# A chunked delta-rule recurrence in a transformer kernel: the two batch rows half a chunk apart, the state kept in PSUM, preparation in smaller pieces, and opening state products at full array size

## Chip, cores and metric

The kernel runs on one core of a Trainium2 chip. The metric is the device time of one execution in microseconds (us), as the median of several runs; the profile is one further execution, taken by the hardware profiler. The engines are TensorE (PE, its weight loads PEld), VectorE (DVE), ScalarE (ACT), GpSimd (POOL) and SyncE (SP, which issues the DMAs).

## What is computed

A two-layer network in float32 over x of shape (2, 1024, 128). Its first part, which the change touches, is a gated delta-rule attention with 8 heads (keys of 64, values of 128). Its core is a scan over the 1024 steps:

```python
def step(S, ins):
    q_t, k_t, v_t, a_t, b_t = ins
    read = jnp.einsum('bhk,bhkv->bhv', k_t, S)
    err = read - v_t
    S = a_t[:, :, None, :] * S - b_t[:, :, None, None] * k_t[..., None] * err[:, :, None, :]
    o_t = jnp.einsum('bhk,bhkv->bhv', q_t, S)
    return (S, o_t)
```

q, k and v come from projections with a causal convolution of 4 taps and SiLU; a and b are sigmoids of projections; the output o is normalised per head, gated and projected. Mixture-of-experts layers, a softmax attention and layer norms follow, which the change leaves alone.

## The kernel before

**Stages.** An opening stage loads and prepares (0 to 71 us of the profile). The recurrence runs from 71 to 1304 us, a short closing stage to 1331 us, and the rest of the network to the end.

**Chunks and segments.** The 1024 steps are cut into 16 segments (f) of 64 steps, each of 4 chunks (c) of 16 steps, each of 4 blocks (i) of 4 steps. There are two batch rows (b = 0, 1); the 8 heads sit side by side in one tile. So there are 64 chunks of each row.

**One row's chunk.** `start` (L637, L644) puts the values and the products of keys and queries with the state into the PSUM bank z of the row. The state products use half of the columns of the array at a time: 8 matmuls with 64 columns of weights. Then come four block steps: `solve` on DVE multiplies z with the small inverse mt (L785) and sums it into w (L788); `turn` transposes w on PE (L653); `keep` on ACT copies 32 rows into wt (L746); `take_off` on PE (L662) takes the block's effect off the later blocks' z. After the fourth, `finish` makes the outputs (L669) and the keys-times-errors product (L677) in PSUM bank 4, one bank for both rows. `update` on DVE scales the outputs (L796), adds bank 4 to the state in SBUF (L799), and multiplies it by the decay (L803), which SP has loaded by DMA. The next chunk's `start` of that row waits for it.

**Products of the keys.** For each chunk and row, `pe_products` (L540, L542) makes the keys' products and their transpose in bank 5; DVE masks them into gq (L574, `dve_masks`) for `take_off` and the outputs, and ACT writes four scaled copies of the transpose into kfull (L552) for L677.

**The ring.** Between the steps of the recurrence the engines do the preparation of the next segment and the normalising, gating and projecting of the last one. The table BOTH has one slot for each of the 16 blocks of a segment, with two parts; a part names items, each one filling of a PSUM bank 6 or 7 by PE (`pe_item`) and its evacuation by ACT (`act_item`) or DVE. The fill of an item waits until the item two before it has been evacuated. a, b, k, q, v are projections (L333, L328), n products of neighbouring keys (L318), g, c, var, rs, wo, yt belong to the last segment.

**Queues.** Every engine works its instructions off in the order in which they are written. The order is written out by hand: for each chunk all four blocks of both rows alternate, with a ring part between them. DVE has its own share of the preparation in `prepare_slot` (L424 to L466), in whole-segment instructions of 256 to 1024 elements a partition; the inverse mt is its last part, ready (m_done) after the last chunk of the segment. POOL goes segment by segment: the scan of the decays (L501), near (L478), rstd, the copies of keys and queries into kq (L492), then the gate (L513, L516).

## Time and profile before

| | us |
|---|---|
| median of 3 runs | 2597.03 (2590.77 to 2597.59) |
| the profiled execution | 2591.12 |
| its span, first to last instruction | 2589.3 |
| the recurrence in it | 1232 (72 to 1304) |
| one segment of 4 chunks | 77 |

The profile shows each engine's busy time, the waits, and the instructions in order of time. PE's busy time counts a pipelined matmul's whole latency, so the distance from one start to the next is what a matmul costs its queue. Each float32 matmul is issued as two passes, a transpose as one; a count of 8 in a row of PE stands for 4 matmuls.

### The profile page before, as it was taken

To read this page: it belongs to the slowest core of one execution; us is meant where nothing else is said; L and a number is where in the kernel's file an instruction comes from. 1 tells how busy PE (TensorE), PEld (TensorE's weight loads), DVE (VectorE), ACT (ScalarE), POOL (GpSimd) and SP (SyncE) were. 2 spreads that over 40 slices of the span, in tenths; PEclk is the share of its full clock that TensorE was granted. 3 is DMA by queue.
4 is the path that set the end of the run, shared out by engine and by line. 5 is a ranking of instruction groups with operands and counts; after the bars stand their busy time and mean duration, and the time that the engine had idled before them with its cause. 6 is when DMAs were issued, how large, how long until landed. Compare 5 with 4: busy or idle time off the path is not lost. (4 is left out here: it accounts for less than half of the span.)

```text
span 2589.3 us, 44842 instructions
## 1 busy us (share of the span) xinstructions
PE 2260.6 (87%) x16524; PEld 1728.4 (67%) x16524; DVE 1531.3 (59%) x3305; ACT 1060.7 (41%) x2983; POOL 457.1 (18%) x868
## 2 busy tenths in 40 slices
PE   4888888888888888888849799999999999969997
PEld 3777777777777777777746556555556656666675
...
DMA packets 76174, 54.81 MB, mean 21 GB/s; under 512 B 6201, under 2 KB 72897, under 8 KB 74945
## 3 DMA queue, kind: packets, MB, share of 16 engines
...
q14 instruction: 73, 0.59, 0.1%
...
## 5 line engine op out<-in xcount | busy, mean ns | idle before, releaser
L1410 DVE TENSOR_REDUCE b_nmax<-ps 128x1 f32<-128x1024 f32 (+7 forms) x256 | 194.1, 758 | 325.0 <-PE ps L1310 324.2
L1306 PE MATMUL ps<-b_kT,b_qT 64*128 64x512 f32 (+3 forms) x768 | 327.8, 535 | 17.3 <-issue 15.4
L1377 ACT ACTIVATE b_prob<-ps,b_nmax 128x1024 f32<-128x1024 f32 (+7 forms) x256 | 189.7, 741 | 342.3 <-DVE b_nmax L1410 342.2
L785 DVE TENSOR_TENSOR prod<-ps,mt 128x128 f32<-128x128 f32 x512 | 148.4, 290 | 294.2 <-PE ps L662 242.7
L328 PE MATMUL ps<-xT,taps 128*128 128x128 f32 x2176 | 299.0, 280 | 0.6 <-ACT vd L379 0.6
L501 POOL TENSOR_TENSOR di<-di 128x128 f32<-128x128 f32 x240 | 130.4, 543 | 786.1 <-DVE di L430 768.5
L328 PEld LDWEIGHTS ps<-xT,taps 128*128 128x128 f32 x2176 | 265.1, 191 | 4.3 <-ACT vd L379 0.9
L653 PE MATMUL ps<-ident,w 128*128 128x128 f32 x512 | 159.7, 312 | 108.1 <-DVE w L788 106.6
L746 ACT COPY wt<-ps 32x128 f32<-32x128 f32 x512 | 129.3, 255 | 242.9 <-PE ps L653 235.4
L1306 PEld LDWEIGHTS ps<-b_kT,b_qT 64*128 64x128 f32 x768 | 127.2, 191 | 120.0 <-issue 103.2
L1039 PE MATMUL ps<-xTn,f_w 128*128 x352 | 167.4, 611 | 24.9 <-PEq L948 18.5
L1053 PEld LDWEIGHTS ps<-f_w,f_hT 128*128 128x128 f32 x1408 | 167.6, 193 | 31.6 <-issue 24.0
L1423 DVE COPY b_probT<-ps 128x512 f32<-128x512 f32 (+3 forms) x256 | 150.2, 587 | 62.0 <-PE ps L1332 60.8
L653 PEld LDWEIGHTS ps<-ident,w 128*128 128x128 f32 x512 | 75.4, 147 | 165.4 <-DVE w L788 161.9
L1332 PE MATMUL ps<-ident,b_prob 128*128 128x128 f32 x1152 | 175.3, 281 | 1.6 <-ACT b_prob L1377 0.9
L677 PE MATMUL ps<-wt,kfull 128*128 128x128 f32 x1024 | 147.7, 290 | 30.1 <-issue 30.1
L1053 PE MATMUL ps<-f_w,f_hT 128*128 128x128 f32 x1408 | 169.3, 277 | 0.8 <-DVE f_hT L1116 0.8
L552 ACT ACTIVATE kfull<-ps,pair_rows 128x128 f32<-128x128 f32 x520 | 162.9, 365 | 15.2 <-DVE gq L574 7.6
L1288 POOL COPY b_spread<-b_inv 128x128 f32<-128x128 f32 x128 | 38.0, 297 | 724.8 <-DVE b_inv L1430 724.8
L1349 PE MATMUL ps<-b_probT,b_v 128*64 128x128 f32 x2304 | 155.0, 279 | 4.5 <-DVE b_yT L1440 4.5
L677 PEld LDWEIGHTS ps<-wt,kfull 128*128 128x128 f32 x1024 | 132.1, 201 | 39.0 <-issue 38.7
L1332 PEld LDWEIGHTS ps<-ident,b_prob 128*128 128x128 f32 x1152 | 133.5, 144 | 35.8 <-issue 28.1
...
## 6 DMA issues: line engine op xcount, KB each, us to landing
decay<-ends_dram SPq DMA_DIRECT2D x256, 128.0 KB, 5.0
...
```

What stands on the lines that cost most here:

```text
L328: mm = pe.matmul(part, lhsT=taps[:, tap, t * P:(t + 1) * P], rhs=xT[:, :, columns(at_next) - LOOK + tap:columns(at_next) - LOOK + tap + TS ...
L552: nc.scalar.activation(kfull[:, B * (cc % 2) + b, g, :], ps[:, 5, KT_AT:KT_AT + P], ACT.Copy, scale=cst["pair_rows"][:, g:g + 1]).then_inc ...
L653: pe.transpose(ps[:, 2 + b, 0:P], w[:, b, :, :, :].rearrange("p i h s -> p (i h s)"), cst["ident"][:, :]).then_inc(wt_ready[b], 1)
L677: mm = pe.matmul(ps[:, 4, g * P:(g + 1) * P], lhsT=kfull[:, n % 4, g, :], rhs=wt[:, b, :], start=True, stop=True, skip_group_check=True)
L1039: pe.matmul(ps[:, m % 4, :], lhsT=w1[:, m * P:(m + 1) * P], rhs=xT[:, bass.ts(part(E // NE), 512)], start=True, stop=True).then_inc(sems[" ...
L1053: mm = pe.matmul(ps[:, 4 + e % 2, t * P:(t + 1) * P], lhsT=hT[:, e % 2, j, t * P:(t + 1) * P], rhs=w2[:, first[e] + j, :], start=(j == 0), ...
L1306: mm = pe.matmul(bank[:, 0:c1 - c0], lhsT=qT[rows, f, b * T + i * P:b * T + (i + 1) * P], rhs=kT[rows, f, b * T + c0:b * T + c1], start=Tr ...
L1332: mm = pe.transpose(ps[:, 4 + j // 4, (j % 4) * P:(j % 4 + 1) * P], prob[:, u % 2, j * P:(j + 1) * P], cst["ident"][:, :])
L1349: pe.matmul(ps[cols, 6, 0:P], lhsT=v[:, f, b * TT + j, cols], rhs=probT[:, (2 * w + h) % 4, j, :], start=(j == 0), stop=(j == i), skip_gro ...
L1377: nc.scalar.activation(prob[:, u % 2, 0:n], src, ACT.Exp, bias=nmax[:, u % 4:u % 4 + 1], accum_out=total[:, w % 4, h:h + 1]).then_inc(sems ...
L1410: nc.vector.tensor_reduce(nmax[:, u % 4:u % 4 + 1], src, axis=AX.X, op=ALU.max, negate=True).then_inc(sems["max_done"], 1)
L1423: nc.vector.tensor_copy(probT[:, u % 4, 0:k, :], ps[:, 4, 0:k * P].rearrange("p (j t) -> p j t", j=k)).then_inc(sems["pt_kept_v"], 1)
```

## The change

- The two rows are half a chunk apart. The loop runs over 128 half chunks, 8 to a segment (j = 0 to 7). In each, one row x makes its `start` and blocks 0 and 1, the other row y its blocks 2 and 3 and its `finish`.
- Each row has its own PSUM bank, 4 or 5, and the state stays in it: L677's products are added onto it (now L699), one DVE instruction multiplies bank by decay into SBUF (L827 takes the place of L799 and L803), and ACT copies the result back into the bank (`put_back`, L774, 128x512).
- The state products of `start` (now L668) are 4 matmuls with all 128 columns of weights instead of 8 with 64.
- The products of the keys are ring items p0 to p7, one to a half chunk. ACT copies their transpose once (kt), and POOL makes kfull from it in one 128x512 instruction with two inputs (L569).
- The ring has 32 parts, in another order. On DVE the preparation is cut in 22 pieces of half the size (`dve_piece`). The diagonal of mt goes from DVE (L438) to ACT, in two halves (L502), the scaling of the values from DVE (L461) to POOL (L510).
- POOL's work of a segment is spread over the halves: near in j = 1, the scan from j = 3, the gate in j = 5, the copies in j = 6, the values in j = 7, and a kfull ahead of each.

```diff
+        BOTH = [["k0.0"], ["k0.1"], ["k1.0"], ["k1.1", "p0"], ["a0"], ["c0"], ["a1"], ["c1", "p1"],
+                ["a2", "var.0"], ["var.1", "b0"], ["b1", "a3"], ["b2", "b3", "p2"], ["n0", "n1"], ["g0", "n2"], ["g1", "n3"],
+                ["p3"], ["rs0", "q0.0"], ["q0.1", "rs1"], ["q1.0"], ["q1.1", "p4"], ["v0.0"], ["v0.1"], ["v1.0"],
+                ["v1.1", "p5"], ["v2.0"], ["v2.1"], ["dt", "v3.0"], ["v3.1", "p6"], ["wo.0"], ["wo.1"], [], ["p7", "yt"]]
         POST = ("g0", "g1", "c0", "c1", "var", "rs0", "rs1", "wo", "yt")
+        PRODUCTS = tuple(f"p{j}" for j in range(2 * NC))
...
+            elif kind == "p":
+                cc, b = product_of(f, int(j))
+                if cc % NC == 0 and cc:
+                    pe.wait_ge(S["copied"], 16 * (cc // NC))
+                keys = kq[:, cc // NC % 2, b, cc % NC, :, :, :, :, :].rearrange("p q i g h s -> p (q i g h s)")
+                pe.matmul(out[:, 0:2 * P], lhsT=keys[:, 0:P], rhs=keys, start=True, stop=True, skip_group_check=True)
+                mm = pe.transpose(out[:, 2 * P:3 * P], keys[:, 0:P], cst["ident"][:, :])
...
+            elif kind == "p":
+                cc, b = product_of(f, int(j))
+                n = B * cc + b
+                act.wait_ge(S["g_kept"], n)
+                if n >= 3:
+                    act.wait_ge(S["k_kept"], n - 2)
+                last_one = nc.scalar.copy(kt[:, n % 2, :], out[:, 2 * P:3 * P])
...
+            if 8 <= q < 12 or 13 <= q < 16:
+                decays_piece(dve, ch, ring, f, nx, q - 8 if q < 12 else q - 13, 0 if q < 12 else 1)
+            if q in (12, 19):
+                rates_piece(dve, ch, ring, f, q // 19)
+            if 20 <= q < 25:
+                inverse_piece(dve, ch, ring, f, nx, q - 20, 0)
+            if 25 <= q < 30:
+                inverse_piece(dve, ch, ring, f, nx, q - 25, 1)
...
+            if step == 0:
+                wait_kept(dve, ring, f, "n3" if half else "n1")
+                dve.wait_ge(S["r_made"], 2 * f + half + 1)
                 ch.step(tt(NN[:, :, 0:3], NN[:, :, 0:3], R[:, :, 1:4], ALU.mult))
-            if slot == 12:
-                tt(NN[:, :, 3:5], NN[:, :, 3:5], R[:, :, 2:4], ALU.mult)
+                ch.step(tt(NN[:, :, 3:5], NN[:, :, 3:5], R[:, :, 2:4], ALU.mult))
+            if step == 1:
                 ch.step(tt(NN[:, :, 5:6], NN[:, :, 5:6], R[:, :, 3:4], ALU.mult))
-            if slot == 13:
-
-                nc.vector.scalar_tensor_tensor(out=M[:, :, 4:16:5], in0=NN[:, :, 0:3], scalar=-1.0, in1=R[:, :, 0:3],
-                                               op0=ALU.mult, op1=ALU.mult)
-
-                dve.wait_ge(S["copied"], 16 * (f + 1))
+                ch.step(stt(out=M[:, :, 4:16:5], in0=NN[:, :, 0:3], scalar=-1.0, in1=R[:, :, 0:3], op0=ALU.mult, op1=ALU.mult))
...
+        def act_diagonal(act, f, nx, half):
+
+            blocks = slice(half * HB * NBLK // 2, (half + 1) * HB * NBLK // 2)
+            act.wait_ge(S["r_made"], 2 * f + half + 1)
+            R = rr[:, :, :, :].rearrange("p h b (n i) -> p (h b n) i", i=BK)[:, blocks]
+            M = mt[:, nx, blocks, :, :].rearrange("p n i j -> p n (i j)")
+            nc.scalar.copy(M[:, :, 0:16:5], R).then_inc(S["diag_made"], 1)
+
+        def pool_values(pool, ring, f, nx):
+
+            wait_kept(pool, ring, f, "v3")
+            pool.wait_ge(S["d_done"], f + 1)
+            inv = di[:, 1, :, :]
+            vv = vd[:, nx, :, :, :].rearrange("p h b (c t) -> p (h b c) t", t=CH)
+            nc.gpsimd.tensor_tensor(vv[:, :, 1:CH], vv[:, :, 1:CH], inv[:, :, 0:CH - 1], ALU.mult).then_inc(S["prepared"], 1)
...
+        def pool_keys(pool, cc, b):
+            n = B * cc + b
+            if cc >= 2:
+                pool.wait_ge(p_ready[b], cc - 1)
+            nc.gpsimd.tensor_tensor(kfull[:, n % 4, :, :], kt[:, n % 2, :].unsqueeze(1).to_broadcast([P, G, P]),
+                                    cst["pair_rows"][:, :].unsqueeze(2).to_broadcast([P, G, P]), ALU.mult).then_inc(
+                S["k_kept"], 1)
...
-                        for half in halves_of_v:
-                            mm = pe.matmul(zo[half, :, g, :], lhsT=state[:, b, g, half],
-                                           rhs=kq[:, f % 2, b, c, :, :, g, :, :].rearrange("p q i h s -> p (q i) (h s)"),
-                                           start=False, stop=(g == G - 1), skip_group_check=True)
+                        mm = pe.matmul(zo[:, :, g, :], lhsT=state[:, b, g, :],
+                                       rhs=kq[:, f % 2, b, c, :, :, g, :, :].rearrange("p q i h s -> p (q i) (h s)"),
+                                       start=False, stop=(g == G - 1), skip_group_check=True)
...
+                    if n >= 1:
+                        pe.wait_ge(S["k_kept"], n)
                     if cc >= 1:
-                        pe.wait_ge(S["k_kept"], 4 * (nth(cc, b) + 1))
-                    for bb in range(B):
-                        if finished[bb]:
-                            pe.wait_ge(p_used[bb], finished[bb])
+                        pe.wait_ge(s_back[b], cc)
                     for g in range(G):
-                        mm = pe.matmul(ps[:, 4, g * P:(g + 1) * P], lhsT=kfull[:, n % 4, g, :], rhs=wt[:, b, :],
-                                       start=True, stop=True, skip_group_check=True)
+                        mm = pe.matmul(ps[:, 4 + b, g * P:(g + 1) * P], lhsT=kfull[:, n % 4, g, :], rhs=wt[:, b, :],
+                                       start=False, stop=True, skip_group_check=True)
                     mm.then_inc(p_ready[b], 1)
...
+                    y, cy = 1 - x, cc - 1 + x
+                    start(cc, x)
+                    if cy >= 0:
+                        turn(cy, y, 2)
+                    ring(0)
+                    if cy >= 0:
+                        take_off(cy, y, 2)
+                    turn(cc, x, 0)
+                    ring(1)
+                    take_off(cc, x, 0)
+                    if cy >= 0:
+                        turn(cy, y, 3)
+                    ring(2)
+                    turn(cc, x, 1)
+                    if cy >= 0:
+                        finish(cy, y)
+                    take_off(cc, x, 1)
+                    ring(3)
+                turn(last_chunk, 1, 2)
+                take_off(last_chunk, 1, 2)
+                turn(last_chunk, 1, 3)
+                finish(last_chunk, 1)
...
+                for cc, x, f, j in halves:
+                    nx = 1 - f % 2
+                    if j or f:
+                        of, oj = (f, j - 1) if j else (f - 1, 2 * NC - 1)
+                        wait_kept(pool, both, of, f"p{oj}")
+                        pool_keys(pool, *product_of(of, oj))
+                    if j == 1:
+                        pool_prepare(pool, both, f, nx, "near")
+                    if j == 3:
+                        pool_rstd(pool, ch, both, f)
+                        scan(ch, nc.gpsimd.tensor_tensor, f, nx)
+                    if j == 5:
+                        pool_gate(pool, ch, both, f)
+                    if j == 6:
+                        pool_prepare(pool, both, f, nx, 0)
+                        pool_prepare(pool, both, f, nx, 1)
+                    if j == 7:
+                        pool_values(pool, both, f, nx)
...
+                def put_back(cc, b):
+                    act.wait_ge(s_ready[b], cc + 1)
+                    nc.scalar.copy(ps[:, 4 + b, :].rearrange("p (g v) -> p g v", g=G), state[:, b, :, :]).then_inc(s_back[b], 1)
...
+                    y, cy = 1 - x, cc - 1 + x
+                    if cy >= 0:
+                        keep(cy, y, 2)
+                    ring(0)
+                    keep(cc, x, 0)
+                    if cc >= 1:
+                        put_back(cc - 1, x)
+                    ring(1)
+                    if j in (4, 6):
+                        act_diagonal(act, f, 1 - f % 2, j // 6)
+                    if cy >= 0:
+                        keep(cy, y, 3)
+                    ring(2)
+                    keep(cc, x, 1)
+                    ring(3)
...
+                def update(cc, b):
                     dve.wait_ge(p_ready[b], cc + 1)
-                    nc.vector.tensor_tensor(state[:, b, :, :], ps[:, 4, :].rearrange("p (g v) -> p g v", g=G),
-                                            state[:, b, :, :], ALU.add).then_inc(p_used[b], 1)
-                    dve.wait_ge(p_used[b], cc + 1)
                     dve.wait_ge(decay_in[b][cc % DS], 32 * (cc // DS + 1))
-                    nc.vector.tensor_tensor(state[:, b, :, :], state[:, b, :, :], decay[:, cc % DS, b, :, :],
-                                            ALU.mult).then_inc(s_ready[b], 1)
-
-                for cc, (f, c) in enumerate(chunks):
-                    def work(i):
-                        dve_slot(dve, ch, both, f, 1 - f % 2, NB * c + i, f - 1)
-
-                    solve(cc, 0, 0)
-                    solve(cc, 1, 0)
-                    work(0)
-                    solve(cc, 0, 1)
-                    dve_masks(dve, cc + 1, 0)
-                    solve(cc, 1, 1)
-                    work(1)
-                    solve(cc, 0, 2)
-                    solve(cc, 1, 2)
-                    work(2)
-                    solve(cc, 0, 3)
-                    dve_masks(dve, cc + 1, 1)
-                    solve(cc, 1, 3)
-                    prepare_slot(dve, ch, both, f, 1 - f % 2, NB * c + NB - 1)
-                    update(cc, 0)
-                    update(cc, 1)
-                    work(3)
-                    if c == NC - 1:
-                        prepare_slot(dve, ch, both, f, 1 - f % 2, 16)
+                    nc.vector.tensor_tensor(state[:, b, :, :], ps[:, 4 + b, :].rearrange("p (g v) -> p g v", g=G),
+                                            decay[:, cc % DS, b, :, :], ALU.mult).then_inc(s_ready[b], 1)
...
+                    y, cy = 1 - x, cc - 1 + x
+                    if cy >= 0:
+                        solve(cy, y, 2)
+                    solve(cc, x, 0)
+                    piece(0)
+                    if cy >= 0:
+                        solve(cy, y, 3)
+                    solve(cc, x, 1)
+                    piece(1)
+                    if cy >= 0:
+                        outputs(cy, y)
+                    piece(2)
+                    if cy >= 0:
+                        update(cy, y)
+                    dve.wait_ge(S["ring_done"], both.done(f, f"p{j}"))
+                    pc, pb = product_of(f, j)
+                    dve_masks(B * pc + pb, bank(both, f, f"p{j}"))
+                    piece(3)
```

**POOL, the recurrence, a segment in the middle.** Before, from the scan to the gate:

```order
L501 TENSOR_TENSOR di<-di 128x128 x15
L478 TENSOR_TENSOR near<-qk 128x128x3
L478 TENSOR_TENSOR near<-qk 128x128x2
L478 TENSOR_TENSOR near<-qk 128x128
L508 TENSOR_SCALAR rstd<-var 128x8
L509 TENSOR_TENSOR rstd<-rstd,minus_half 128x8
L492 COPY kq<-qk 64x8x4x4 x16
L513 TENSOR_SCALAR gate<-gate 128x1024
L516 TENSOR_TENSOR cs<-cs,gate 128x512 x2
```

The same engine now, from the scan (L544) to the values (L510); L535 are the copies, L556 and L559 the gate:

```order
L544 TENSOR_TENSOR di<-di 128x128 x15
L569 TENSOR_TENSOR kfull<-kt,pair_rows 128x512 x2
L556 TENSOR_SCALAR gate<-gate 128x1024
L559 TENSOR_TENSOR cs<-cs,gate 128x512 x2
L569 TENSOR_TENSOR kfull<-kt,pair_rows 128x512
L535 COPY kq<-qk 64x8x4x4 x16
L569 TENSOR_TENSOR kfull<-kt,pair_rows 128x512
L510 TENSOR_TENSOR vd<-vd,di 128x64x15
```

Eight kfull instructions and the values have come in, and the gate stands behind the scan and two of them.

**DVE, the end of a chunk in which part of the inverse is made.** Before:

```order
L788 TENSOR_REDUCE w<-prod 128x32
L438 COPY mt<-rr 128x256x4
L439 TENSOR_TENSOR gn<-gn,rr 128x256x3
L796 TENSOR_TENSOR vd<-ps,di 128x8x16
L799 TENSOR_TENSOR state<-ps,state 128x512
L803 TENSOR_TENSOR state<-state,decay 128x512
L796 TENSOR_TENSOR vd<-ps,di 128x8x16
L799 TENSOR_TENSOR state<-ps,state 128x512
L803 TENSOR_TENSOR state<-state,decay 128x512
```

Now, half chunk j = 5 of a segment, from its first piece of the inverse to the next half's first solve (L811, L814 are `solve`, L821 the outputs, L827 the update, L574 the masks):

```order
L477 TENSOR_TENSOR gn<-gn,rr 128x128x3
L478 TENSOR_TENSOR gn<-gn,rr 128x128x2
L811 TENSOR_TENSOR prod<-ps,mt 128x128
L814 TENSOR_REDUCE w<-prod 128x32
...
L483 TENSOR_TENSOR tmp<-gn,rr 128x128x2
L484 TENSOR_TENSOR tmp<-gn,mt 128x128x2
L827 TENSOR_TENSOR state<-ps,decay 128x512
L574 TENSOR_TENSOR gq<-ps,head_masks 128x256
L486 SCALAR_TENSOR_TENSOR mt<-tmp 128x128x2
L487 TENSOR_TENSOR tmp<-gn,rr 128x128
L811 TENSOR_TENSOR prod<-ps,mt 128x128
```

Each piece now stands between two solves, and one of them (L486, L487) between the masks and the half's first solve.

**PE, one row's start.** Before, two rows one behind the other; now one, followed by the other row's turn (L677 is now `turn`):

```order
L637 MATMUL ps<-vd,ident 128x128
L644 MATMUL ps<-kq,state 64x8x8 x8
```

```order
L662 MATMUL ps<-vd,ident 128x128
L668 MATMUL ps<-kq,state 128x8x8 x4
L677 MATMUL ps<-ident,w 128x128
```

The eight half-width products have become four of full width.

## Rows read from the trace of the kernel before

**Rows 1.** Windows: length; busy us of PE, PEld, DVE, ACT, POOL; clock, DMA share.
```profile
640.00:717.00 77.00, 66.94 (x563) 59.49 (x562) 53.66 (x120) 37.84 (x119) 22.19 (x38) 0.93 0.12 29
72.00:1304.00 1232.00, 1065.43 (x9055) 941.71 (x9054) 867.63 (x1936) 605.58 (x1904) 364.46 (x624) 0.95 0.13 29
```

**Rows 2.** Timeline of PE: runs of passes, each up to the next's start.
```profile
640.56 1.84 PE L286 MATMUL ps<-mean_col,gn 128*128 128x1 f32 x16
642.27 0.31 PE L653 MATMUL ps<-ident,w 128*128 128x128 f32 x1
...
647.63 0.69 PE L644 MATMUL ps<-kq,state 128*64 128x64 f32 x16
648.25 1.16 PE L328 MATMUL ps<-xT,taps 128*128 128x128 f32 x8
```

**Rows 3.** Waits in the recurrence: who waited for whom, us, times, longest.
```profile
DVE prod L785 <- PE ps L662: 242.7, 256, 2.5
DVE state L799 <- PE ps L677: 36.5, 80, 1.4
PE ps L653 <- DVE w L788: 106.6, 153, 2.1
```

**Rows 4.** Timeline, one block step: start, us, engine, line, instruction.
```profile
653.31 0.29 DVE L785 TENSOR_TENSOR prod<-ps,mt 128x128 f32<-128x128 f32 x1
653.64 0.29 DVE L788 TENSOR_REDUCE w<-prod 128x32 f32<-128x128 f32 x1
653.98 0.33 PE L653 MATMUL ps<-ident,w 128*128 128x128 f32 x1 [0.24 <-DVE w L788]
654.34 0.26 ACT L746 COPY wt<-ps 32x128 f32<-32x128 f32 x1 [0.28 <-PE ps L653]
656.09 0.31 PE L662 MATMUL ps<-gq,wt 128*128 128x32 f32 x2
656.43 0.29 DVE L785 TENSOR_TENSOR prod<-ps,mt 128x128 f32<-128x128 f32 x1 [0.79 <-PE ps L662]
```

**Rows 5.** Groups of the recurrence on DVE: count, busy us, mean ns, idle before.
```profile
L799 DVE TENSOR_TENSOR state<-ps,state 128x512 f32<-128x512 f32 x128 | 88.0, 688 | 36.5 <-PE ps L677 36.5
L574 DVE TENSOR_TENSOR gq<-ps,head_masks 128x256 f32<-128x256 f32 x128 | 54.1, 422 | 8.5 <-PE ps L542 7.9
L445 DVE SCALAR_TENSOR_TENSOR mt<-gn,rr 128x768 f32<-128x768 f32 x16 | 24.7, 1542 | 0.0
L441 DVE TENSOR_TENSOR gn<-gn,rr 128x512 f32<-128x512 f32 x16 | 14.0, 873 | 0.0
L442 DVE TENSOR_TENSOR gn<-gn,rr 128x256 f32<-128x256 f32 x16 | 10.1, 633 | 0.0
```

**Rows 6.** Timeline of DVE and POOL where both read SBUF.
```profile
53.34 1.00 DVE L439 TENSOR_TENSOR gn<-gn,rr 128x768 f32<-128x768 f32 x1
...
657.93 2.78 POOL L513 TENSOR_SCALAR gate<-gate 128x1024 f32<-128x1024 f32 x1 [1.72 <-DVE cs L403]
...
660.55 1.12 DVE L438 COPY mt<-rr 128x1024 f32<-128x1024 f32 x1
660.79 3.83 POOL L516 TENSOR_TENSOR cs<-cs,gate 128x512 f32<-128x512 f32 x2
661.51 1.99 DVE L439 TENSOR_TENSOR gn<-gn,rr 128x768 f32<-128x768 f32 x1
```

**Rows 7.** ACT: a projection with a table load, and a copy of 128x512.
```profile
689.99 1.28 ACT L384 ACT_TABLE_LOAD   x1
691.28 0.37 ACT L384 ACTIVATE ex<-ps,bias_a 128x128 f32<-128x128 f32 x1
...
630.87 0.59 ACT L360 COPY cs<-ps 128x512 f32<-128x512 f32 x1 [2.48 <-PE ps L312]
```

**Rows 8.** The page's DMA issues: count, KB each, median us to landing.
```profile
decay<-ends_dram SPq DMA_DIRECT2D x256, 128.0 KB, 5.0
```

**Rows 9.** One line of POOL: shortest, median and longest of an instruction in ns.
```profile
L516 POOL TENSOR_TENSOR cs<-cs,gate x34: 1262/1902/1983, 122.5 to 1325.0; 128x512 f32<-128x512 f32 x34
```

295 lines of the change are left out of this document (114 added, 181 removed), and 3 rows, old and new, of the table BOTH.

## Prediction

> **What bounds the kernel now.** I read the windows first. The recurrence takes 1232 us, 16 segments of 77 us [rows 1]; what follows it is untouched. PE looks nearly full by its busy time, 66.9 of 77 [rows 1], but its starts say otherwise. 16 passes of L286 stand between 640.56 and 642.27, so a pass costs 0.107 us even where it moves one column; 16 half-width state passes take 0.62 us, from 647.63 to 648.25 [rows 2]. In a segment of before I count 402 passes of full weights and up to 128 columns (128 for q, k, v, 80 for a, b, g, var and wo, 32 turns, 48 for take_off, 80 in `finish`, 34 others) at 0.11, 44.6 us; the eight starts' state products at 0.62 to 0.72, 5.8; and about 8 us for the wider ones (c, n, the products of the keys): 58 us of PE in 77. DVE is busy 53.7, ACT 37.8, POOL 22.2 [rows 1]. So no engine is full; what ends last is a handover of the recurrence. DVE waited 242.7 us for `take_off` and 36.5 for the shared bank 4, PE 106.6 us for w [rows 3]. One block step, from rows near each other [rows 4]: solve 0.33 to the second instruction's start and 0.29, so 0.62; PE takes w 0.05 later; 0.36 to ACT's start (I take 0.40 where the weights' load doesn't coincide); 0.26 for the copy; 0.05; 0.45 from `take_off`'s load to DVE (0.34 from its matmul, 656.09 to 656.43, and 0.11 for the load): 1.83 us.
>
> **What the change removes.** On DVE one of the two 0.69 us state instructions [rows 5], 8 x 0.69 = 5.5 us a segment, with the wait for the shared bank, and the copy L438, 1.12 us [rows 6], and the scaling of the values. On ACT the kfull copies; put_back comes in, by the nearest row, a 128x512 copy, 0.59 us [rows 7]. The lockstep goes: while one row waits, the other's steps and the ring stand in between. The decays' way out (item dt, the store, the loads of 5.0 us [rows 8]) starts at part 27 of 32 instead of slot 13 of 16, a sixteenth of a segment later, 4 to 5 us, and the first decay is needed at the end of the second half after the border, over 20 us on: nothing.
>
> **What it adds.** (1) State products: 8 passes at 0.107 to 0.11, 0.86 to 0.89 us for 0.62 to 0.72: +0.2 us, 128 times on PE. PE then has 59.5 us a segment, 7.4 a half chunk.
> (2) Halving DVE's preparation does not halve its time. 512 elements in groups took 0.87 us, 256 took 0.63 [rows 5]: about 0.38 fixed, so 128 take 0.49; L445's kind with 384 is (1.54 - 0.35)/2 + 0.35 = 0.95. The five pieces of the inverse come to 1.35, 1.5, 1.4, 1.25 and 2.05 us, 7.55 for a half of the heads, 15.1 a segment; from the same rows taken whole it is some 12. With 32 solves of 0.55 to the next instruction, 17.6, outputs 2.0, updates 5.6, masks 3.4 and the other pieces 10, DVE has 53.7: what it saved is eaten.
> (3) POOL gets eight kfull and the values. 128x512 with two inputs took at least 1.26 us [rows 9], so 1.24 to 1.3 each, and 2.3 for 960 elements; 22 us become 35.
> (4) From bank to next `start` DVE has 0.7 us instead of 1.4.
>
> **A half chunk, step by step.** Zero is the start of PE's identity product. PE is done with `start` at 1.11, z is there at 1.26. DVE may mask only when the products item, last in the ring's last part, is made (0.2), so until 0.62; then comes a piece, then solve(y,2), only then solve(x,0). PE's order then adds: turn 0.11, ring part, take_off 0.22, turn, ring part, take_off, turn, ring part, turn, output product 0.22, state product 0.89, take_off 0.22, last ring part. From the third ring part's end to the last one's start that is 1.45 us. Where the third part isn't what ends last, it is the solve or ACT's keep.
> j=0: DVE comes 0.8 late from the half before, so the first turn is at 2.15; three parts of 0.89 (8 passes); last part 1.44: 8.5.
> j=1: ACT decides. Item a0 holds the table load, th and 1.28 and ex and two more, 2.56 us [rows 7], and row x's keep stands behind it, to 4.6; put_back 0.59 and c0 1.1 before row y's keep, to 6.4; a1 (1.1) before x's next, to 7.6: 9.25.
> j=2: two a items and four b on ACT, parts of 1.33 on PE, and the products wait for b2's copy: 9.3. j=3: 8.4.
> j=4: keep 4.5, put_back 5.1, table load 6.4, q0 7.0; q1 on PE waits for q0's copy: 10.8.
> j=5: no wait for ACT. Pieces of 1.1, 1.35, 1.5, 1.4: turn at 2.4, PE's order gives 8.7; DVE's update ends 0.8 later. j=6: masks to 1.2, a piece of 1.25, turn at 3.05; the piece of 2.05 puts y's last solve at 6.15, the third part ends at 7.3: 10.2. j=7: 8.2.
> Sum: 73.4 us a segment, 3.6 under 77, if DVE and POOL never meet.
>
> **Where they meet.** L439 took 1.00 us alone and 1.99 beside L516 [rows 6]; L516, 1.26 at its shortest, took 1.90 in the median [rows 9]. L516 begins at 660.79 under the copy L438, L439 at 661.51 under L516: each time the second goes on when the first ends. DVE instructions with an input in PSUM aren't among them in what I place here (masks, solves, outputs, update); the pieces are.
> In j=5 the gate now stands where the first pieces of the inverse are. POOL's kfull ends at 2.96, L477 (0.6) goes to 3.55, then L513 takes its 2.78 [rows 6] to 6.3, and L478 (0.6) follows; solve(y,3) is done at 7.4 instead of 4.8, and PE idles. The two L516 (now L559) hold the next piece: 11.35 instead of 8.7. That L513, with one tensor input, holds DVE as L516 does is not in the trace; between 0 and 2.75 us I take the whole, by the nearest row, L516. In j=6 a kfull slips between the two instructions of the piece ahead of solve(y,2), +1.25, the copies cost some 0.5, and DVE starts late: 12.45 for 10.2. In j=7 again, and the values (2.3) on one piece: 9.8 for 8.2. Together +6.5: 79.9 us a segment.
>
> The Trainium skill speaks against this move to POOL: its page SBUF — State Buffer, section SBUF: two separate sides, has an exclusive lock, for the whole instruction, between a GpSimd instruction and a VectorE one in a two-port mode or with two SBUF inputs. L439 and L516 agree (1.99 for 1.00, 1.90 for 1.26). By that rule L513 holds the pair too, as in my sum; were it not so, the third rival's 77.1 would stand.
>
> **Sum.** 16 x 79.9 = 1278; the last row's second half has nothing beside it, two block steps, finish and update, +5: 1283 for 1232, +51. The opening stage: the inverse in 15.1 instead of 12 us after the scan, +3. The closing stage has the same work: 0. The profiled execution took 2591.1, so 2645; it stands 5.9 under the median, which becomes **2651**.
>
> **Rivals.**
> One, faster: the queues of DVE and POOL slide apart, the gate between two pieces, a kfull while DVE waits for PE. For it: a half of j=0 to 4 leaves DVE 3 us and more of waiting. Against it: in j=5 to 7 DVE has 8 to 9.7 us of work in a half of 9. It decides from the point at which the pieces find POOL idle. 73.4 x 16 + 5 + 3 is 1182, -50 us: 2547.
> Two, much faster: the offset of half a chunk hides ACT and DVE wholly, and PE ends last: 59.5 and 2.5 of gaps, 62 x 16 + 8, -232: 2365. Against it stand the table loads and the order masks, piece, solve.
> Three: L513 doesn't hold DVE, j=5 is 2.75 shorter: 77.1 x 16 + 8, +10: 2607, at the edge of no change.
> Four, slower still: the clock. The recurrence had 0.95 of it, this segment 0.93 [rows 1], so PE was at the lower of its two levels (1.2 and 2.4 GHz) about a tenth of the time. With idle stretches of 2 to 3 us in j=5 to 7 it could do most of its 22 us there at 1.2 GHz; what shows of that, with POOL falling behind, I put at +3 a segment: 2700.
>
> **How the numbers follow.** Forecast 0.48, rival one 0.22, two 0.05, three 0.13, four 0.12. A measurement can tell some 0.3%, 8 us, from no change. Faster: one, two and a little of the edge, 0.29. Within: most of three, 0.12. Slower: 0.59. The range reaches from one to four with the doubt of each sum (0.8 us a segment is 13 us): 2540 to 2715, which leaves rival two and the tails out. The likeliest case alone is 2625 to 2680.
>
> **What would show it.** Right: segments of about 80 us; L477 or L478 at 2 to 3 us in the median instead of 0.6; L556, L559 or L569 longer than alone; the table load at L403 ahead of a late keep; PE idle ahead of L677 with DVE's w as releaser; L668 at 0.11 a pass. Wrong: L477 to L492 at their lengths alone and segments near 73, or PE's idle time gone and 62. If segments are near 80 with short pieces, the cause is ACT's order or the clock and not the ports.

## The result: 40 us slower, and the profile after

| | before | after |
|---|---|---|
| median of 4 runs, us | 2597.3 (2590.8 to 2598.3) | 2637.6 (2630.0 to 2638.0) |
| ratio of the times | | 1.0154 (95% interval 1.0129 to 1.0179) |
| span of the profiled execution, us | 2589.3 | 2636.1 |
| recurrence, us | 71.3 to 1304.6 = 1233.3 | 77.9 to 1356.6 = 1278.7 |
| PE's mean granted clock over the span | 0.942 | 0.942 |

The predicted time was 2651 us. Of the 46.8 us between the two spans 45.4 are in the recurrence (51 forecast), 6.6 in the opening stage (3), -3.0 in the closing stage (0), and the rest of the network gives back 2.

The windows of one segment after, one line for each half chunk j = 0 to 7 (a half begins with PE's identity product L662), the whole recurrence, and the page's line of busy times. They answer to [rows 1]:

```profile
core 0: us, PE busy (x) PEld busy (x) DVE busy (x) ACT busy (x) POOL busy (x), PEclk, DMA share, GB/s
720.51:728.10 7.59, 7.55 (x67) 7.32 (x66) 3.92 (x13) 2.75 (x10) 1.04 (x1) 1.00 0.16 38
728.10:739.12 11.02, 9.12 (x48) 6.59 (x46) 3.62 (x11) 6.96 (x20) 2.77 (x4) 0.85 0.10 25
739.12:748.89 9.77, 9.18 (x76) 8.41 (x74) 5.99 (x16) 7.23 (x25) 1.04 (x1) 1.00 0.11 30
748.89:757.23 8.34, 8.34 (x68) 8.11 (x66) 5.73 (x17) 4.83 (x12) 3.49 (x3) 1.00 0.12 29
757.23:768.33 11.10, 9.20 (x75) 8.34 (x74) 6.69 (x16) 5.06 (x12) 8.29 (x16) 1.00 0.01 1
768.33:777.55 9.22, 7.72 (x68) 7.33 (x66) 8.71 (x17) 3.05 (x12) 6.94 (x4) 1.00 0.01 2
777.55:790.47 12.92, 10.00 (x69) 8.91 (x68) 10.53 (x24) 4.34 (x14) 5.61 (x17) 0.87 0.01 3
790.47:799.63 9.16, 6.36 (x52) 5.80 (x51) 8.59 (x19) 2.33 (x9) 3.71 (x2) 1.00 0.49 114
78.00:1357.00 1279.00, 1086.37 (x8033) 984.28 (x8034) 860.26 (x2080) 584.22 (x1678) 525.01 (x767) 0.95 0.13 28
```

```profile
PE 2279.8 (86%) x15501; PEld 1767.0 (67%) x15501; DVE 1525.7 (58%) x3465; ACT 1041.3 (39%) x2753; POOL 619.8 (24%) x1013
```

The halves are unequal: 7.6 to 12.9 us. Again no engine is full. j=6 stands out: DVE is busy 10.5 of 12.9 us, and PE's clock is 0.87.

The waits of the whole recurrence after (us in total, times, longest). They answer to [rows 3]:

```profile
DVE prod L811 <- PE ps L686: 151.8, 159, 2.9
DVE gq L574 <- PE ps L300: 95.7, 80, 2.7
DVE vd L821 <- PE ps L692: 92.9, 84, 1.9
DVE state L827 <- PE ps L699: 27.9, 32, 1.4
PE ps L677 <- DVE w L814: 101.5, 114, 1.6
```

DVE's wait for `take_off` fell from 242.7 to 151.8 us. Its wait for the state's products in bank 4, 36.5 us, is 27.9 in the rows' own banks. But new waits stand in their place: 95.7 us for the products of the keys, the last item in PE's ring (7.9 in before), and 92.9 us for the output product L692 (0.8 in before). In sum DVE waits 381 us in the recurrence after and 334 before, while its busy time is about the same (860.3 and 867.6). PE's wait for w went from 106.6 only to 101.5. No wait of PE, DVE or ACT in the recurrence is put down to an instruction of POOL by the profile, so where POOL costs time it is by stretching DVE's instructions and not by being late itself.

### The profile page after: what moved, and what is told of

Same layout as the page of the kernel before. It is cut to its first block and busy times, and to the rows that moved or that the text cites. A ratio compares the mean times of both kernels' runs of the same rounds, so it can differ in the third digit from the quotient of the medians.

```text
span 2636.1 us, 43056 instructions
## 1 busy us (share of the span) xinstructions
PE 2279.8 (86%) x15501; PEld 1767.0 (67%) x15501; DVE 1525.7 (58%) x3465; ACT 1041.3 (39%) x2753; POOL 619.8 (24%) x1013
## 5 line engine op out<-in xcount | busy, mean ns | idle before, releaser
L341 PE MATMUL ps<-xT,taps 128*128 128x128 f32 x2176 | 315.1, 290 | 20.6 <-ACT qk L394 18.5
L341 PEld LDWEIGHTS ps<-xT,taps 128*128 128x128 f32 x2176 | 289.8, 205 | 30.7 <-ACT qk L394 21.5
L569 POOL TENSOR_TENSOR kfull<-kt,pair_rows 128x512 f32<-128x512 f32 x128 | 148.2, 1158 | 638.9 <-ACT kt L369 536.7
L677 PE MATMUL ps<-ident,w 128*128 128x128 f32 x512 | 162.9, 318 | 104.0 <-DVE w L814 101.5
L811 DVE TENSOR_TENSOR prod<-ps,mt 128x128 f32<-128x128 f32 x512 | 147.3, 288 | 167.1 <-PE ps L686 151.8
L1066 PE MATMUL ps<-xTn,f_w 128*128 x352 | 167.4, 611 | 24.9 <-PEq L975 18.5
L677 PEld LDWEIGHTS ps<-ident,w 128*128 128x128 f32 x512 | 95.4, 186 | 129.5 <-DVE w L814 124.7
L686 PEld LDWEIGHTS ps<-gq,wt 128*128 128x128 f32 x768 | 127.5, 206 | 47.3 <-ACT wt L770 45.4
L668 PE MATMUL ps<-kq,state 128*128 128x64 f32 x1024 | 133.9, 274 | 28.1 <-DVE state L827 28.1
L814 DVE TENSOR_REDUCE w<-prod 128x32 f32<-128x128 f32 x512 | 146.5, 286 | 17.5
## 6 DMA issues: line engine op xcount, KB each, us to landing
wtap<-in_taps SPq DMA_DIRECT2D x4, 1024.0 KB, 11.3
```

Source lines behind the costliest of these rows:

```text
L341: mm = pe.matmul(part, lhsT=taps[:, tap, t * P:(t + 1) * P], rhs=xT[:, :, columns(at_next) - LOOK + tap:columns(at_next) - LOOK + tap + TS ...
L569: nc.gpsimd.tensor_tensor(kfull[:, n % 4, :, :], kt[:, n % 2, :].unsqueeze(1).to_broadcast([P, G, P]), cst["pair_rows"][:, :].unsqueeze(2) ...
L677: pe.transpose(ps[:, 2 + b, 0:P], w[:, b, :, :, :].rearrange("p i h s -> p (i h s)"), cst["ident"][:, :]).then_inc(wt_ready[b], 1)
L811: ch.step(nc.vector.tensor_tensor(prod[:, b, :, :, :], zi, mtc[:, :, b, NB * c + i, :, :], ALU.mult))
L1066: pe.matmul(ps[:, m % 4, :], lhsT=w1[:, m * P:(m + 1) * P], rhs=xT[:, bass.ts(part(E // NE), 512)], start=True, stop=True).then_inc(sems[" ...
```

## Where the segments' time is

The mean length of each half, worked out as the mean distance between the identity products of `start` over the segments, beside the forecast and three of the runs below:

| j | forecast | after | POOL cut (e1) | filler (e12) | five edits (e11) |
|---|---|---|---|---|---|
| 0 | 8.5 | 7.7 | 7.7 | 7.7 | 7.9 |
| 1 | 9.25 | 10.7 | 10.2 | 9.6 | 8.5 |
| 2 | 9.3 | 10.1 | 10.0 | 10.2 | 9.1 |
| 3 | 8.4 | 8.3 | 8.3 | 8.3 | 8.8 |
| 4 | 10.8 | 11.2 | 11.2 | 11.2 | 9.6 |
| 5 | 11.35 | 9.2 | 8.6 | 9.2 | 8.0 |
| 6 | 12.45 | 13.0 | 9.6 | 11.8 | 10.6 |
| 7 | 9.8 | 9.2 | 7.8 | 10.5 | 7.8 |
| sum | 79.9 | 79.4 | 73.4 | 78.6 | 70.2 |

The sum was right and the halves were not: j=5 is 2.1 us shorter than forecast, j=1 1.5 us longer. DVE and POOL in j=5 of the segment shown, the timeline (start, us, engine, line):

```profile
770.97 1.37 DVE L477 TENSOR_TENSOR gn<-gn,rr 128x384 f32<-128x384 f32 x1
772.38 0.52 DVE L478 TENSOR_TENSOR gn<-gn,rr 128x256 f32<-128x256 f32 x1
773.98 1.29 DVE L480 TENSOR_TENSOR gn<-gn,rr 128x128 f32<-128x128 f32 x1
775.30 1.80 DVE L481 SCALAR_TENSOR_TENSOR mt<-gn,rr 128x384 f32<-128x384 f32 x1
778.54 0.69 DVE L827 TENSOR_TENSOR state<-ps,decay 128x512 f32<-128x512 f32 x1
...
793.24 2.49 DVE L486 SCALAR_TENSOR_TENSOR mt<-tmp 128x256 f32<-128x256 f32 x1
...
770.88 2.77 POOL L556 TENSOR_SCALAR gate<-gate 128x1024 f32<-128x1024 f32 x1
773.74 2.66 POOL L559 TENSOR_TENSOR cs<-cs,gate 128x512 f32<-128x512 f32 x2
```

L477, 0.56 us elsewhere, takes 1.37 beside the gate addition L556, but L478 runs at its own 0.52 beside the same instruction; both are so in all 16 segments. L480 (0.39 elsewhere) and L481 (0.84) both stretch beside the products L559. These 2.7 us put `update` L827 at 778.54, a microsecond after j=6 began. PE in j=6, the timeline with idle time before in brackets, shows what follows:

```profile
777.55 0.43 PE L662 MATMUL ps<-vd,ident 128*128 128x128 f32 x2
779.28 1.10 PE L668 MATMUL ps<-kq,state 128*128 128x64 f32 x8 [1.31 <-DVE state L827]
781.97 0.33 PE L677 MATMUL ps<-ident,w 128*128 128x128 f32 x1 [1.58 <-DVE w L814]
782.13 1.18 PE L341 MATMUL ps<-xT,taps 128*128 128x128 f32 x8
783.63 1.92 PE L341 MATMUL ps<-xT,taps 128*128 128x128 f32 x8
```

PE idles 1.31 us for the late state and 1.58 for w, and then the same 8 passes that take 1.06 in other halves take 1.18 and 1.92: the granted clock has fallen to the lower level (1.2 of 2.4 GHz) for a stretch. In j=7 L486, the last DVE row above, took 2.49 us where it takes 0.59, beside POOL's values L510:

```profile
793.03 2.25 POOL L510 TENSOR_TENSOR vd<-vd,di 128x960 f32<-128x960 f32 x1
```

The DVE groups of the recurrence after (count, busy, mean ns) have both kinds in one mean, two of each a segment. They answer to [rows 5]:

```profile
L486 DVE SCALAR_TENSOR_TENSOR mt<-tmp 128x256 f32<-128x256 f32 x32 | 49.4, 1543 | 0.0
L481 DVE SCALAR_TENSOR_TENSOR mt<-gn,rr 128x384 f32<-128x384 f32 x32 | 42.5, 1328 | 1.1
L477 DVE TENSOR_TENSOR gn<-gn,rr 128x384 f32<-128x384 f32 x32 | 30.9, 964 | 0.6 <-issue 0.2
L480 DVE TENSOR_TENSOR gn<-gn,rr 128x128 f32<-128x128 f32 x32 | 26.9, 840 | 0.0
L487 DVE TENSOR_TENSOR tmp<-gn,rr 128x128 f32<-128x128 f32 x32 | 24.8, 775 | 1.1
```

## Experiments

Each was timed beside the kernel before on the same chip; "against after" takes the difference of the medians to 2637.6. The before of those runs stood at 2590.4 to 2592.9, 5 us lower than beside after, so differences under about 8 us decide nothing here.

### Does POOL hold DVE? (e1, e6, e9)

```diff
-            ch.step(nc.gpsimd.tensor_scalar(gate[:, :], gate[:, :], 1.0, None, ALU.add))
+            ch.step(nc.gpsimd.tensor_scalar(gate[:, 0:2 * size], gate[:, 0:2 * size], 1.0, None, ALU.add))
...
-            nc.gpsimd.tensor_tensor(kfull[:, n % 4, :, :], kt[:, n % 2, :].unsqueeze(1).to_broadcast([P, G, P]),
+            nc.gpsimd.tensor_tensor(kfull[:, n % 4, :, 0:4], kt[:, n % 2, 0:4].unsqueeze(1).to_broadcast([P, G, 4]),
```

The diff shows one line of each kind. e1 cuts kfull, the whole gate and the values together; e6 kfull alone; e9 the gate addition L556 alone. Each cuts POOL's instructions to a few columns and so leaves a part of the computation out; waits, signals and the other engines' work stay.

> The changed kernel with POOL's long instructions in the recurrence cut to a few columns (kfull to 4 of 128, the gate's two kinds to 16 columns, the values to one group of 64), so a part of the computation is left out; every wait, signal and all of the other engines' work stays. Theory P (ports): in a segment DVE's pieces are held some 5.0 us by POOL (L477 0.7, L480 0.9, L481 0.9, L486 1.8, L487 0.7), most of it in halves 5 to 7, where DVE's order sets the end. Expected 3.5 to 5 us a segment less: 55 to 80 us under the changed kernel, near 2570. L486 falls from a mean of 1.51 to 0.6 us. Theory A (ACT's order and PE's own work set the end in all halves): under 10 us less.

> The kernel after, with POOL's products kfull cut from 128 columns to 4 in each instruction (the rest of the buffer stays zero; what L699 adds is then not the state's update); the gate and the values stay on POOL in full. An earlier run with all three cut (kfull, gate, values) took 2545.7, 92 us less than after. Theory K (the eight kfull a segment are what meets DVE's pieces and what the late update hangs on): most of the 92 comes back here, 2555 to 2580, and L477, L480 and L487 are at their medians in nearly all segments, while L486 is still held by the values (2.24 us) in j=7. Theory V (the gate and the values, of 2.8, 2 x 1.26 and 2.24 us, are the costly meetings): less than a third comes back, 2607 to 2630, with j=6 near 12.5 and j=7 near 9.

> The kernel after, with POOL's gate addition L556 (one tensor input, 128x1024, 2.77 us) cut to 16 columns; the rest of the gate's additions is left out, and the two products L559 stay whole. The forecast took it that this instruction holds DVE's pieces in j=5 for its whole length, 2.75 us a segment, 44 us in all. Theory G (it does hold them, only elsewhere than where I placed it): -25 to -44 us against after, 2593 to 2612. Theory N (an instruction with one input holds nothing, as L478 at 0.52 us beside it suggests; POOL has only 2.7 us less to do, and the products L559 and the next kfull come 2.7 us earlier, to meet other pieces): within 12 us of after, 2625 to 2649.

| run | median, us | ratio to before | against after |
|---|---|---|---|
| e1 all three | 2545.7 | 0.9826 (0.9809 to 0.9843) | -92 |
| e6 kfull | 2584.8 | 0.9978 (0.9953 to 1.0003) | -53 |
| e9 gate addition | 2597.1 | 1.0022 (1.0009 to 1.0034) | -41 |

With POOL out of the way a segment is 73.4 us, to the tenth what the forecast's step-by-step sum gave for "DVE and POOL never meet". That it agrees to the tenth is luck, since the halves differ from that sum by -0.8 to +1.0 us and cancel. But since nobody waits for POOL, the 6 us a segment between e1 and after are what POOL's instructions do to DVE's, with what hangs on it: some 1.8 of them are the lower clock's, if a half's cost is read as in e12 below (j=6 13.0 at 0.87 and 11.8 filled; j=1 and j=2 together 0.6 shorter in e1). Theory G's number came in e9, but not by its mechanism. The same stretch of e9, where the gate addition takes 0.25 us:

```profile
741.06 0.55 DVE L477 TENSOR_TENSOR gn<-gn,rr 128x384 f32<-128x384 f32 x1
741.64 1.47 DVE L478 TENSOR_TENSOR gn<-gn,rr 128x256 f32<-128x256 f32 x1
744.19 0.39 DVE L480 TENSOR_TENSOR gn<-gn,rr 128x128 f32<-128x128 f32 x1
744.61 0.86 DVE L481 SCALAR_TENSOR_TENSOR mt<-gn,rr 128x384 f32<-128x384 f32 x1
746.93 0.69 DVE L827 TENSOR_TENSOR state<-ps,decay 128x512 f32<-128x512 f32 x1
...
741.31 2.85 POOL L559 TENSOR_TENSOR cs<-cs,gate 128x512 f32<-128x512 f32 x2
```

L477 is back at 0.55, which shows that it was L556 that stretched it. The gate's products now meet L478 instead of L480 and L481, one hold instead of two. j=5 is no shorter (9.3 us), but `update` stands at 746.93, ahead of j=6's start at 747.75, and j=6 drops from 13.0 to 10.4 us. The Trainium skill (SBUF — State Buffer, SBUF: two separate sides) has the lock of the shared port pair held for the whole instruction; the two-input L559 and L510 agree (L480 1.29 for 0.39, L486 2.49 for 0.59), while the one-input L556, which reads SBUF too, cost L477 0.8 us and L478 nothing. There the measurement decides against the Trainium skill; why L556 held the one and not the other stays open.

### Whole pieces instead of halved ones (e5)

```diff
-            if 20 <= q < 25:
-                inverse_piece(dve, ch, ring, f, nx, q - 20, 0)
-            if 25 <= q < 30:
-                inverse_piece(dve, ch, ring, f, nx, q - 25, 1)
+            if 20 <= q < 30:
+                whole_piece(dve, ch, ring, f, nx, q)
```

> The kernel after, with one edit: the inverse on DVE is made in ten whole pieces (both halves of the heads in each instruction) instead of two times five pieces of half the size, at the same ten places q = 20 to 29. By the rows of before such whole instructions took some 10.2 us a segment where nothing held them; in after the halved ones take 12.3 by their medians and, with what POOL holds, some 17. Theory S (the halving of DVE's instructions is a part of what the change loses): 2 us less DVE work in j=5 to j=7, where DVE's queue sets the pace, of which half to all shows, and fewer instructions to be caught by POOL: -15 to -35 us against after, 2605 to 2622. Rival (DVE's length in these halves does not matter, POOL's holds do): within 6 us of after, since a longer instruction is held just as long. A second rival: a whole piece is too long to stand between two solves, the later row's turn comes 0.5 us later in each of ten parts: slower than after by 20 to 60 us.

2592.8 us, ratio 1.0006 (0.999 to 1.0021): -45, more than theory S's best (-35). Both rivals fall. Of the 2.8 us a segment, j=6 has 2.6 (10.4 us, at a clock of 1.00 in all 15 listed), and the other seven halves together are 0.2 us shorter than after's. So 2 us less for DVE do not come back piece by piece, as theory S had it, but almost all through the one half.

### Is j=6 the clock's? (e12)

e1, e5, e6 and e9 all bring j=6 from 13.0 us to 9.6 to 11.2, and their savings do not add up: the 53 of e6 and the 41 of e9 are already the 92 of e1, which leaves nothing for the gate's products and the values. The windows of j=6 (us, PE busy, clock), three segments of after, then of e9:

```profile
777.55:790.47 12.92, 10.00 (x69) 0.87 0.01 3
856.57:869.93 13.36, 10.12 (x69) 0.87 0.01 2
935.13:948.52 13.39, 10.13 (x69) 0.87 0.01 2
```

```profile
747.75:758.09 10.34, 8.30 (x69) 1.00 0.02 4
823.03:833.36 10.33, 8.28 (x69) 1.00 0.01 3
...
1127.86:1139.21 11.35, 9.55 (x68) 0.85 0.02 4
```

All 15 windows of after read 0.86 or 0.87; of e9's, 14 read 1.00 and the one shown last 0.85. The length goes with the clock. e12 therefore adds work: PE makes transposes nobody reads, where it idled.

```diff
+                def fill(n):
+                    for _ in range(n):
+                        pe.transpose(ps[:, 2, 2 * P:3 * P], cst["ident"][:, :], cst["ident"][:, :])
...
+                    start(cc, x, 8 if j == 6 else 0)
+                    fill(12 if j == 6 else 0)
...
                     ring(1)
+                    fill(12 if j == 1 else 0)
                     take_off(cc, x, 0)
```

> The kernel after, with work added: PE makes 8 transposes of the identity into an unused piece of PSUM ahead of j=6's wait for the state, 12 behind that half's start, and 12 in j=1 ahead of the take_off that waits behind the table load (32 a segment, some 3.4 us of PE at 0.107, 55 us in all). In after PE idles in these three places, 1.31, 1.58 and 1.45 us in the segment f=8, and the granted clock shows 0.87 in all 15 of the j=6 halves that I listed, which take 12.6 to 13.4 us; where an edit elsewhere (whole pieces, kfull light, gate addition light) left the clock at 1.00 in j=6 it took 10.3 to 10.8. Likewise j=1 takes 9.69 at 1.00 and 11.0 to 12.0 at 0.76 to 0.85, and j=2 9.77 and 11.07. Theory C (the clock falls because PE has stood idle, and the lost time is the lower clock's): with the idle time filled the clock stays at 1.00, j=6 takes 10.4 to 11, j=1 9.7 and j=2 9.8: -2 to -3.9 us a segment, 2575 to 2605, although PE has more to do. Theory D (the 13 us of j=6 are DVE's and POOL's lateness, the clock only goes with it): no gain, 2637 to 2650, and where the filler outlasts the idle time up to 2660.

2632.3 us, ratio 1.0152 (1.013 to 1.0173) for after's 1.0154: a segment is 0.8 us shorter, and the time as good as the same. The windows of e12 show why both theories are half right. First j=6, then j=1, then j=7:

```profile
764.21:776.01 11.80, 10.79 (x89) 1.00 0.01 3
843.53:855.33 11.80, 10.81 (x89) 1.00 0.02 4
...
716.16:725.83 9.67, 9.03 (x59) 1.00 0.12 27
794.12:803.80 9.68, 9.04 (x60) 1.00 0.13 29
...
776.01:786.56 10.55, 7.76 (x52) 0.86 0.45 101
855.33:866.00 10.67, 7.87 (x52) 0.84 0.58 98
```

In the two halves that were filled theory C holds: the clock stays at 1.00 in every segment, j=1 takes 9.67 us where it took 9.69 to 12.00, and j=6 11.8 where it took 13.0, although PE has 32 transposes more to make in the two halves, 3.4 us by an estimate of 0.107 each. But the fall only moves. In after j=7 ran at 1.00 in 9.2 us; now it runs at 0.85 in 10.5, with the same idle stretches ahead of w (1.17 and 1.43 us for 1.17 and 1.45 in after). j=2, which was not filled, stays at 10.2 us and falls in 6 of its 16 windows (4 in after), where theory C had 9.8. Nor does the longest idle stretch of a half decide: e9's j=6, at 1.00, has one of 1.80 us ahead of w, after's has 1.31 and 1.58. The remaining 11.8 us of j=6 against e9's 10.4, both at full clock, are the late update's (PE still waits 0.45 us for the state and 0.27 for w behind the fillers, so these delay nothing). So of the 2.6 us between after and e9 in j=6 about 1.2 are the clock's and 1.4 the lateness's. That the clock's part would come back if the idle time went in the next halves too is not shown.

### The last piece behind the solves (e4)

```diff
+                    late_piece(f, j)
...
-                    piece(3)
```

> The changed kernel with DVE's last piece of a half moved behind the next half's two first solves, nothing else. Theory O (the order masks, piece, solve delays PE's first turn by a piece, 0.7 to 1.25 us, in halves 4 to 7): up to 1 us less in four halves, 30 to 60 us less, PE's wait for w of 97 us falls by half. Rival: the piece only comes later, ahead of the next solve; DVE's work is the same and ends last in halves 5 to 7: within 15 us.

2665.4 us, ratio 1.0284 (1.0267 to 1.0301): +28, which neither theory had. j=6 does fall to 10.6 us, but j=5 rises to 10.7, and j=7 to 11.2 at a clock of 0.85 (9.2 at 1.00 in after): the piece now stands ahead of the second solves, and PE waits 121.7 us for w instead of 101.5.

### The state products at full width (e3, e7)

e3 puts the half-width products back into after; e7 puts the full-width ones into before.

```diff
-                        for half in halves_of_v:
-                            mm = pe.matmul(zo[half, :, g, :], lhsT=state[:, b, g, half],
+                        mm = pe.matmul(zo[:, :, g, :], lhsT=state[:, b, g, :],
```

> The changed kernel with the opening state products of before, 8 matmuls with 64 columns of weights instead of 4 with 128. Full width measured 0.97 us for 8 passes against 0.62 to 0.72 for 16 half-width ones. If PE's own work ends last in the light halves: up to 0.3 us less in five to eight of eight halves, 1.5 to 2.4 us a segment, 24 to 38 us less. If the start of a half is waited for by nobody (DVE's masks, piece and solve end later): under 8 us less.

> The kernel before, with one part of the change alone: each chunk's opening state products as 4 matmuls with all 128 columns of weights instead of 8 with 64. In before the two rows run in lockstep and both starts of a chunk stand one behind the other on PE. The forecast's first term prices such a start at +0.2 to +0.3 us (0.97 us for 0.62 to 0.72), 128 times; if PE ends last around the chunk's start, that is +26 to +38 us: 2619 to 2631. Theory H (the start is hidden behind DVE's masks, as the half-width version of the changed kernel, which took the same time as after, suggests): within 8 us of before, 2589 to 2601, and PE's idle time ahead of the first turn of a chunk shrinks by as much as the start grows.

e3: 2637.5, no change. e7: 2614.6, ratio 1.008 (1.0051 to 1.0108), +22 beside its own before. The same part costs nothing in one kernel and nearly the lower end of its bound, 26 us, in the other. The price is a little above the forecast's 0.86 to 0.89 us: L668's 8 passes stand between 728.33 and 729.30, 0.97 us for 0.62 [rows 2]. In after the first turn of a half waits for DVE's w, whose solve stands behind masks and a piece; with the shorter start PE's wait for w only grew, from 96.9 to 130.5 us with the half-width products, both between 75 and 1340. In before DVE's solve waits for `start`: that wait went from 41.5 to 55.1 us in e7 (both between 75 and 1300), and a segment from 76.8 to 78.2. Some of e7's segments also show a clock of 0.89 to 0.93 where all of before's show 0.94 to 0.96, so a part of the 22 us can be the clock's; how much was not separated.

### The table loads (e2, e10)

```diff
+                if j in "03":
+                    run(early[:, :], cst["eps"][:, :], ACT.Exp if j == "0" else ACT.Silu)
```

> The changed kernel with one short Exp after k1's copy and one short Silu ahead of p3's copy on ACT, so that the two table loads of a segment stand where ACT waits for DVE's masks (0.4 to 2.1 us idle there) and no longer ahead of a keep in half 1 and of q0 in half 4. Theory A: 1.28 us less in each of the two halves, 2.5 us a segment, 40 us less, 2597; half 1 from 10.9 to 9.6 and half 4 from 11.1 to 9.9 us. Theory P alone (ports): under 10 us less, as the time lost is DVE's.

> The kernel before, with one-column activations that load ACT's two tables ahead of the items that need them (behind wo and behind c1). In after the same edit brought 33 us (2.1 us a segment), since two keeps and a fill waited behind the loads. If the late tables are the offset's own price (in lockstep the loads lie in ACT's waits): within 8 us of before, 2584 to 2600. If they cost every order the same: -25 to -40 us, 2552 to 2567, and the version e8 at 2550 owes nothing to the offset.

e2: 2604.2, ratio 1.0052 (1.0032 to 1.0071), -33. e10: 2616.7, ratio 1.0086 (1.0058 to 1.0115), +26 beside its own before. The halves of e2 are not as theory A had them: j=1 falls by 2.2 us, j=4 by 1.0 and j=6 by 1.3, while j=5 rises by 1.4, at a clock of 0.85 in 9 of its 16, and j=2 by 0.6. So the late tables are a price of the new order and not of every order, and ACT in j=1 of after is what the forecast laid out, step for step:

```profile
730.11 0.37 ACT L402 ACTIVATE th<-ps,bias_a 128x128 f32<-128x128 f32 x1 [0.19 <-PE ps L346]
730.49 1.28 ACT L403 ACT_TABLE_LOAD   x1
731.78 0.37 ACT L403 ACTIVATE ex<-ps,bias_a 128x128 f32<-128x128 f32 x1
732.55 0.24 ACT L770 COPY wt<-ps 32x128 f32<-32x128 f32 x1
...
732.84 0.41 PE L686 MATMUL ps<-gq,wt 128*128 128x32 f32 x2 [1.45 <-ACT wt L770]
```

That the early load makes before slower I had not expected. Its second chunk of a segment is 1.5 us longer (20.0 for 18.5) and its segments show clocks down to 0.91; which of its ring places causes it was not tried.

### Three edits, and five (e8, e11)

e8 joins e2 and e5 and scales the values on DVE (1.15 us there, 2.24 on POOL). e11 moves two things more:

```diff
-                ["a2", "var.0"], ["var.1", "b0"], ["b1", "a3"], ["b2", "b3", "p2"], ["n0", "n1"], ["g0", "n2"], ["g1", "n3"],
-                ["p3"], ["rs0", "q0.0"], ["q0.1", "rs1"], ["q1.0"], ["q1.1", "p4"], ["v0.0"], ["v0.1"], ["v1.0"],
+                ["a2", "var.0"], ["var.1", "b0"], ["b1", "a3"], ["b2", "p2"], ["n0", "n1"], ["g0", "n2"], ["g1", "n3"],
+                ["b3", "p3"], ["rs0", "q0.0"], ["q0.1", "rs1"], ["q1.0"], ["q1.1", "p4"], ["v0.0"], ["v0.1"], ["v1.0"],
...
-            if q in (12, 19):
-                rates_piece(dve, ch, ring, f, q // 19)
+            if q in (12, 17):
+                rates_piece(dve, ch, ring, f, q // 17)
```

> The kernel after, with three edits: one-column activations ahead of ACT's two table switches load the tables in its idle time (alone -33 us), the inverse on DVE in ten whole pieces, and the scaling of the values on DVE as a last piece (0.9 to 1.2 us) instead of on POOL (2.24 us, which held a DVE piece in j=7). If the three causes are apart from each other: 2637 - 33 - 25 - 15 = 2564, 33 us under before. If they overlap (all of them remove lateness of the same halves, j=6 and j=7, and the clock's fall in them): 2585 to 2605, no better than before. If only the kfull products matter beside the tables: 2600 or more.

> The version e8 (early tables, whole pieces of the inverse, values on DVE), with two more edits: DVE's second rates piece stands at q = 17 in j=4 (where DVE waits for PE) instead of q = 19, whose place is ahead of j=5's first solve, where L467 and L468 took 2.33 us beside a kfull; and item b3 goes from the last part of j=2, where the products item waits for ACT's copies of b2 and b3, to the last part of j=3. If the two places are what ends last there: j=5 from 10.8 to 9.0 and j=2 from 10.1 to 9.4, 2.5 us a segment, 2510 to 2525. If the kfull that meets the rates piece only meets the next piece instead: within 10 us of e8, 2540 to 2560.

e8: 2550.3 us, ratio 0.9834 (0.9809 to 0.9859), -87. That is below the 2564 expected for causes apart from each other, but only since whole pieces stood there at -25 and e5 found -45; -33 and -45 are 78 of the 87. e11: 2493.4, ratio 0.9622 (0.9603 to 0.9642), 97 us under its own before and 144 under after, more than was expected. Its halves are in the table: j=5 went from 10.8 in e8 (9.8 where the clock stayed at 1.00) to 8.0, now that no piece stands ahead of its first solves, j=2 from 10.1 to 9.1. Its segment of 70.2 us is 6.6 under before's 76.8, so the change as a whole is worth having once DVE, ACT and POOL are placed for it. How much of that is the rows' offset and how much the state in PSUM, which spares DVE one of two state instructions, no run separates.

## Why the prediction came out right, and where it was not

The mechanism named (the change gains 3.6 us a segment, and DVE and POOL lose 6.5 where they meet) is what the runs show in the sum: 73.4 us without the meetings (e1; 73.4 forecast, 76.8 in before), 79.4 with them (79.9). Where the meetings cost their time was forecast wrong, and the closeness of the sums is luck: the halves miss by up to 2.1 us either way. Of the signs named, segments near 80, kfull longer than alone (1.53 for 1.04), the table load ahead of a late keep and PE idle ahead of w came; L477 or L478 at 2 to 3 us in the median did not (1.37 in one half of each segment, 0.56 in the other, and 0.52). Point by point:

- **The state products, term (1): near in size, wrong in place.** 0.97 us for 0.86 to 0.89, but nothing on after's path (e3), since DVE's order masks, piece, solve covers it. The sum of PE's passes has a slip without consequence: 402 at 0.11 are 44.2 us, not 44.6.
- **The halved pieces, term (2): over-sized.** I had 15.1 us a segment. The medians of the twelve instructions (L478 0.52, L480 0.40, L487 0.44 and the others at 0.39 to 0.86) make some 6.15 a half, 12.3 a segment. The fixed part, 0.38 us from L441 and L442 [rows 5], doesn't hold for these strided forms: 128 elements took 0.39, 256 took 0.50. That the halving costs all the same is e5's -45 us. DVE's 53.7 us a segment are found, 53.8, but by luck: the holds are in them, and e1, almost without holds, has 48.3.
- **POOL's items, term (3): kfull over-sized.** L569 takes 1.04 alone, 1.5 beside a piece; I had 1.24 to 1.3. The values took 2.24 for 2.3.
- **The gate in j=5: the step that failed.** I let L513, now L556, hold DVE for its whole length, 2.78 us, and put 2.65 us on j=5 for the gate. L556 held DVE 0.8, and with the gate's products j=5 is 9.2 us for e1's 8.6, so it pays 0.6. Rival three's reason (L513 holds nothing) came nearer; its time, 2607, did not come, because the same holds, through the late update, cost j=6 more than I had there.
- **j=6: 12.45 forecast, 13.0 found, by another cause.** I had a kfull inside a piece (+1.25), the copies (0.5) and DVE's late start. DVE's late start is there, and one kfull (L487 at 1.16 for 0.39); the other microsecond is the clock's. Four edits (e1, e5, e6, e9) each took j=6 under 11.3 us, which shows how near this half stands to an edge.
- **The clock, rival four.** I gave it 0.12 and 3 us a segment on top of the forecast. It is there in j=6 (1.2), j=1 (10.7 in the mean, 9.67 with the filler) and j=2 (9.77 at 1.00 and 11.07 at 0.80), some 2.6 us a segment, an estimate from these differences. Before's recurrence had the same 0.95 as after's, so the clock is not why after is slower than before; my halves, though, were laid out at full clock. It filled the hole that the gate's term left, so the sum came out within 0.5 us a segment by misses that cancel.
- **ACT in j=1 and j=4: right.** 10.8 forecast for j=4, 11.2 found; j=1's 9.25 is 9.69 at full clock.
- **The opening stage: 6.6 for 3.** DVE's first decays piece starts at 45.78, after 20.86 us of waiting for ACT's items, in before the first stands at 38.61, so I take it that the ring's new order brings them late; and the last of its pieces, L492, took 2.34 us beside POOL's values L510, a meeting I hadn't looked for there. The closing stage gave back 3.0 where I had nothing.

The rows of that meeting, DVE and POOL in the timeline of the opening stage, after:

```profile
66.69 2.34 DVE L492 SCALAR_TENSOR_TENSOR mt<-tmp 128x128 f32<-128x128 f32 x1
...
66.55 2.23 POOL L510 TENSOR_TENSOR vd<-vd,di 128x960 f32<-128x960 f32 x1 [0.61 <-POOL kq L535]
```
